# Where a projection's bias is added: a product with one row of ones, or an addition on VectorE while PSUM is emptied

## The chip, the cores and the metric

The kernel runs on one core of a Trainium2 chip. It uses TensorE (PE, with its weight loads shown as PEld), VectorE (DVE), ScalarE (ACT), GpSimd (POOL) and the DMA engines, whose transfers are started by SyncE (SP) and GpSimd. The metric is the device time of one execution in microseconds (us), lower is better.

## The reference, cut to what matters

The program is eight blocks, each added to the node features `x` (3125 nodes, 256 features, float32), over a graph of 53125 edges. Five times in it a matrix of node features is multiplied by a weight matrix and the result stays in node order. Three of the five have a bias, and two of those a rectifier:

```python
h = jnp.einsum('ni,hio->hno', x, W)          # block 0: 256 columns + 8 folded ones, no bias
logits = tokens @ router_w.T                 # block 1: 8 columns, no bias
logits = xt @ Wr + br                        # block 5: 8 columns, bias
h = jax.nn.relu(x @ w1 + b1)                 # block 6, twice: 256 columns, bias, rectifier
msg = ew[:, None] * h[src]                   #   then gathered by edge and summed by node
```

## The kernel before

Nodes lie in 25 tiles of 125 (`T` = 25, `P` = 125), worked through in five groups (`NG`) of five (`GT`). The transposed features `XT` (or `F`) have features on partitions, in `KH` = 2 halves of 128, and nodes along the free dimension.

The program is a sequence of phases (`Phase`), and each ends with a barrier of all engines (L79 to L81), so nothing of one phase overlaps the next. `project` is one such phase. It is called five times: at about 64 us (block 0), 1552 us (block 1), 4691 us (block 5), 5388 us and 6203 us (block 6, first and second convolution). In each call:

- SyncE loads the weights (L514), the bias as one row of one partition (`b_row`, L516), and in block 0 two vectors that are broadcast to 128 partitions (L518).
- VectorE waits for all loads and then copies each node tile of `XT` into one of five slots (L541), since TensorE takes its stationary operand from there. Before it refills a slot it waits until the product that used it is done (`multiplied`).
- TensorE waits for the slot (`slot_ready`) and for its PSUM bank to be free (`kept`), multiplies the two halves (L559), and where there is a bias adds a third product, of a row of ones with the bias row (L562). Each float32 product is two passes, so a tile is four weight loads with four matmul records, and two more of each with a bias. Only then it signals `multiplied`.
- ScalarE waits for `multiplied`, reads the PSUM bank, applies the rectifier or a copy, and writes the tile into `H` or `logits` (L571), and signals `kept`.
- In blocks 0 and 6 SyncE waits for each group of five tiles and stores it to a table in DRAM (L523), 625 KB at a time, and at the end waits until all five stores have landed.

There are five slots and five PSUM banks (`acc`), one for each tile of a group, so up to five tiles may be under way. After the projections of block 6 comes `aggregate`, whose first instruction on VectorE is the clearing of `AT` (L612). After that of blocks 1 and 5 comes the routing of tokens, whose first instruction is an iota on GpSimd (L1131).

`normalize` (L379) makes `XT` and is used below for comparison: in block 2 it stores the same table of 625 KB groups (L411).

Of the kernel before, what the change touches and what calls it, by code (L numbers as in the profile page):

```python
# [23 lines left out]
ALU = mybir.AluOpType  # L24
ACT = mybir.ActivationFunctionType
# [5 lines left out]
P = 125  # L31
T = N // P
CH = E // P
KH = C // 128
GT = 5
NG = T // GT
# [73 lines left out]
def tile(t):  # L110
    return bass.ds(t, 1)


def nodes(t, n=1):
    return bass.ds(t * P, n * P)
# [372 lines left out]
def project(nc, g, XT, weight, out, bias=None, relu=False, table=None, fold=(), att=None):  # L488

    width = weight.shape[-1]
    extra = sum(heads for heads, _ in fold)
    full = width + extra
    with Phase(nc) as ph:
        w = ph.sb("w", [128, KH, full])
        vec = ph.sb("vec", [128, max(len(fold), 1), width])
        prod = ph.sb("prod", [128, width])
        b_row = ph.sb("b_row", [1, width])
        slot = ph.sb("slot", [128, GT, KH, P])  # L500
        acc = ph.psum("acc", [P, GT, 512])
        loaded = ph.sem("loaded")
        folded = ph.sem("folded")
        slot_ready = ph.sem("slot_ready")
        multiplied = ph.sem("multiplied")
        kept = ph.sem("kept")
        stored = ph.sem("stored")
        n_loads = 1 + (bias is not None) + len(fold)
        n_folds = sum(2 * KH for _ in fold)
        block = ph.block()  # L510

        @block.sync
        def _(sp):
            sp.dma_start(w[:, :, 0:width], weight.rearrange("(h p) n -> p h n", p=128)).then_inc(loaded, 16)  # L514
            if bias is not None:
                sp.dma_start(b_row[:], bias).then_inc(loaded, 16)  # L516
            for n, (_, v) in enumerate(fold):
                sp.dma_start(vec[:, n], v.partition_broadcast(128)).then_inc(loaded, 16)  # L518
            if table:
                with sp.Fori(0, NG) as i:  # L520
                    sp.wait_ge(kept, (i + 2) * GT)
                    for dram, lo, n in table:
                        sp.dma_start(dram[bass.ds(i * GN, GN), :].rearrange("(t p) c -> p t c", p=P),  # L523
                                     out[:, bass.ds(i * GT, GT), lo:lo + n]).then_inc(stored, 16)
                sp.wait_ge(stored, 16 * NG * len(table))

        @block.vector
        def _(dve):
            dve.wait_ge(loaded, 16 * n_loads)
            then = Steps(dve, folded)  # L530
            at = width
            for n, (heads, _) in enumerate(fold):
                for h in range(KH):
                    then(dve.tensor_tensor(prod[:], w[:, h, 0:width], vec[:, n], ALU.mult))
                    then(dve.tensor_reduce(w[:, h, at:at + heads], prod[:].rearrange("p (a c) -> p a c", a=heads), AX_X, ALU.add))
                at += heads
            with dve.Fori(0, NG) as i:
                for k in range(GT):

                    dve.wait_ge(multiplied, i * GT + k + 1)  # L540
                    dve.tensor_copy(slot[:, k], XT[:, :, nodes(i * GT + k)]).then_inc(slot_ready, 1)  # L541
            if att is not None:
                dve.wait_ge(kept, GT + T)
                then(dve.tensor_copy(att[:], out[:, :, full - HEADS:full]))

        @block.tensor
        def _(pe):

            pe.sem_inc(multiplied, GT)
            pe.wait_ge(loaded, 16 * n_loads)  # L550
            if n_folds:
                pe.wait_ge(folded, n_folds)
            with pe.Fori(0, NG) as i:
                for k in range(GT):
                    pe.wait_ge(slot_ready, i * GT + k + 1)

                    pe.wait_ge(kept, i * GT + k + 1)
                    for h in range(KH):
                        last = pe.matmul(acc[:, k, 0:full], slot[:, k, h], w[:, h], start=(h == 0),  # L559
                                         stop=(h == KH - 1 and bias is None))  # L560
                    if bias is not None:
                        last = pe.matmul(acc[:, k, 0:width], g.ones[0:1, :], b_row[:], start=False, stop=True)  # L562
                    last.then_inc(multiplied, 1)

        @block.scalar
        def _(act):
            act.sem_inc(kept, GT)
            with act.Fori(0, NG) as i:
                for k in range(GT):
                    act.wait_ge(multiplied, (i + 1) * GT + k + 1)  # L570
                    act.activation(out[:, tile(i * GT + k), :].rearrange("p a c -> p (a c)"), acc[:, k, 0:full],  # L571
                                   ACT.Relu if relu else ACT.Copy).then_inc(kept, 1)


def aggregate(nc, g, table, AT):
# [1885 lines left out]
def build(nc, arrays, begin=0, end=8):  # L2461
# [9 lines left out]
    with ExitStack() as top:  # L2471
# [4 lines left out]
        if begin <= 0 < end:  # L2476
            normalize(nc, g, X, XT)
            with ExitStack() as st:
                a_dst = st.enter_context(nc.sbuf_tensor("a_dst", [P, T, HEADS], F32))
                with ExitStack() as s2:  # L2480
                    H = s2.enter_context(nc.sbuf_tensor("H", [P, T, C + 2 * HEADS], F32))
                    project(nc, g, XT, d["L0_gnn_W"], H, fold=((HEADS, d["L0_gnn_a_src"]), (HEADS, d["L0_gnn_a_dst"])),
                            table=((edge_table, 0, C + HEADS),), att=a_dst)
                attend_edges(nc, g, edge_table, a_dst, d["dst_flat"], dst_row, X)
            count_edges(nc, g, counts, scratch)
        if begin <= 1 < end:
            with ExitStack() as st:
                XN = st.enter_context(nc.sbuf_tensor("XN0", [P, T, C], F32))
                logits = st.enter_context(nc.sbuf_tensor("logits0", [P, T, NX], F32))
                normalize(nc, g, X, XT, XN)  # L2490
                project(nc, g, XT, d["L0_ffn_router"], logits)
                sparse_experts(nc, g, logits, XN, X, scratch, K=2, guard=1e-12, keep=True, hidden=C,
                               **{name: d["L0_ffn_" + name] for name in ("w1", "b1", "w2", "b2")})
# [28 lines left out]
        if begin <= 5 < end:  # L2522
            with ExitStack() as st:
                XN = st.enter_context(nc.sbuf_tensor("XN2", [P, T, C], F32))
                logits = st.enter_context(nc.sbuf_tensor("logits2", [P, T, NX], F32))
                normalize(nc, g, X, XT, XN, twice=True)
                project(nc, g, XT, d["L2_ffn_Wr"], logits, bias=d["L2_ffn_br"])
                sparse_experts(nc, g, logits, XN, X, scratch, K=2, hidden=4 * C, w1=d["L2_ffn_W1"], b1=d["L2_ffn_b1"],
                               w2=d["L2_ffn_W2"], b2=d["L2_ffn_b2"], gain=d["L2_ffn_ln_g"], offset=d["L2_ffn_ln_b"])
# [38 lines left out]
```

## Time and profile before

| | us |
|---|---|
| median of 3 runs | 7331.43 |
| lowest, highest | 7329.41, 7336.07 |
| the profiled execution's own time | 7337.61 |
| its span, first to last instruction | 7336.1 |
| mean granted TensorE clock | 0.768 of 2.4 GHz |

The profile is of one execution. Its busy shares are means over stages that are limited by different engines: TensorE 67%, its weight loads 56%, VectorE 37%, ScalarE 32%, GpSimd 34%. A change in one stage has to be read from that stage. The granted clock is 1.00 at 2.4 GHz and 0.50 at 1.2 GHz.

### The profile page before, as it was taken

How to read it: one execution, taken by the hardware profiler on the slowest of the kernel's cores; microseconds unless marked ns; L12 is line 12 of the kernel's file. 1: busy time of each engine (PE TensorE's matmuls, PEld its weight loads, DVE VectorE, ACT ScalarE, POOL GpSimd, SP SyncE). 2: the span in 40 equal slices, each digit the busy share in tenths (PEclk: the TensorE clock that was granted, in tenths of full speed). 3: DMA queues.
4: the chain of work that ended last, by engine and by line, in shares of the span. 5: the costliest groups of instructions: out<-in, count | busy, mean ns of one | idle time of the engine just before them, and what ended most of it. 6: DMA issues, size and time to landing. Idle time of an engine off the chain costs nothing. (4 is left out here: it accounts for less than half of the span.)

```text
span 7336.1 us, 100226 instructions
## 1 busy us (share of the span) xinstructions
PE 4950.6 (67%) x23535; PEld 4095.8 (56%) x23536; DVE 2728.1 (37%) x5564; ACT 2374.0 (32%) x4829; POOL 2524.9 (34%) x2090
## 2 busy tenths in 40 slices
PE   3878635535357677584989989559757766766746
PEld 2766535523245554483878868558635554555535
DVE  4444535530222212105968879400022222222143
ACT  2333124424211113343656656335311112111132
POOL 3778300022357760201000000030127773577600
PEclk7887769968766668797999989679856666576668
DMA  3333220012223320221111111022113331233300
GB/s 88 95 98 99 73 76 34 34 36 84 69 77 85 85 72 6 76 79 47 57 41 52 43 50 57 10 85 81 53 45 85 85 85 44 68 85 85 76 13 19
DMA packets 360158, 464.62 MB, mean 63 GB/s; under 512 B 191387, under 2 KB 275146, under 8 KB 360074
## 3 DMA queue, kind: packets, MB, share of 16 engines
q0 software_dynamic: 262016, 293.64, 15.8%
q1 hardware_dynamic: 79988, 152.25, 6.0%
q10 hardware_dynamic: 18070, 17.79, 0.9%
q8 instruction: 31, 0.51, 0.0%
q14 instruction: 53, 0.43, 0.0%
HBM read 377.19 MB, written 84.20 MB: 63 GB/s over the span
## 5 line engine op out<-in xcount | busy, mean ns | idle before, releaser
L607 POOL DMA_INDIRECT p_message<-node_table,p_index x1275 | 1554.5, 1219 | 737.0 <-ACT p_index L599 461.4
L641 PE MATMUL p_acc<-p_spread,p_message 125*128 125x160 f32 x5100 | 1357.8, 425 | 644.1 <-DVE p_spread L621 300.0
L641 PEld LDWEIGHTS p_acc<-p_spread,p_message 125*128 125x128 f32 x5100 | 1101.4, 276 | 901.1 <-issue 827.3
L2158 PE MATMUL p_acc<-p_H,p_eT 125*125 125x256 f32 x3750 | 823.5, 378 | 0.0
L1131 POOL IOTA p_order_i<- 125x200 int32 x3 | 1.1, 374 | 2359.0 <-SPq L79 2359.0
L599 ACT COPY p_index<-src_col 125x1 int32 x1275 | 240.5, 191 | 1682.4 <-PE p_acc L641 1508.4
L2158 PEld LDWEIGHTS p_acc<-p_H,p_eT 125*125 125x125 f32 x3750 | 695.0, 187 | 106.0
L886 POOL DMA_INDIRECT p_message<-edge_table,p_index x425 | 562.5, 1324 | 144.9 <-issue 128.0
L627 DVE TENSOR_TENSOR AT<-AT,p_acc 128x320 f32 x75 | 36.6, 488 | 1314.1 <-PE p_acc L641 920.1
L621 DVE TENSOR_SCALAR p_spread<-node_number,dst_value,edge_weight_col 125x160 f32 x1275 | 397.0, 385 | 198.7 <-issue 198.7
L1439 PE MATMUL p_up<-p_xT,p_w1s 128*128 128x125 f32 x3056 | 393.6, 287 | 101.9 <-ACT p_xT L1474 73.3
L1439 PEld LDWEIGHTS p_up<-p_xT,p_w1s 128*128 128x128 f32 x3056 | 379.7, 201 | 133.6 <-ACT p_xT L1474 67.9
L1079 PE MATMUL p_acc<-p_message,p_spread 125*125 125x260 f32 x1666 | 424.4, 421 | 6.7 <-DVE p_message L1013 3.6
L729 PE MATMUL p_acc<-p_cell,p_low 125*125 125x325 bf16 x1250 | 231.6, 337 | 257.0 <-DVE p_cell L707 182.5
L1494 DVE TENSOR_TENSOR p_rows_out<-p_down,p_b2s 125x256 f32<-125x256 f32 x136 | 57.7, 425 | 921.6 <-PE p_down L1448 840.7
L1079 PEld LDWEIGHTS p_acc<-p_message,p_spread 125*125 125x125 f32 x1666 | 347.2, 210 | 79.7 <-issue 12.6
L1448 PE MATMUL p_down<-p_w2s,p_hid 128*125 128x256 f32 x1528 | 364.9, 388 | 3.0 <-ACT p_hid L1479 2.3
L483 PE MATMUL p_turned<-identity,p_slot 125*128 125x125 f32 x400 | 88.9, 374 | 411.0 <-DVE p_slot L451 407.2
L1479 ACT ACTIVATE p_hid<-p_up,p_b1s 128x125 f32<-128x125 f32 x764 | 272.6, 365 | 243.2 <-PE p_up L1439 200.0
L729 PEld LDWEIGHTS p_acc<-p_cell,p_low 125*125 125x125 bf16 x1250 | 176.1, 152 | 284.6 <-issue 230.7
L2081 ACT ACTIVATE p_eT<-p_turned 125x500 f32<-125x500 f32 (+1 forms) x525 | 251.1, 540 | 203.6 <-PE p_turned L2151 187.2
L1448 PEld LDWEIGHTS p_down<-p_w2s,p_hid 128*125 128x125 f32 x1528 | 283.2, 193 | 45.5 <-ACT p_hid L1479 7.5
(400 smaller groups left out, 6913.7 us busy)
## 6 DMA issues: line engine op xcount, KB each, us to landing
p_count<-edge_counts SPq DMA_DIRECT2D x75, 762.9 KB
p_message<-node_table,p_index POOLq DMA_INDIRECT x1275
edge_counts<-p_total SPq DMA_DIRECT2D x25, 762.9 KB
p_rows_in<-dealt ACTq DMA_DIRECT2D x139, 125.0 KB
made<-p_rows_out SPq DMA_DIRECT2D x136, 125.0 KB
p_w1s<-in_L_ffn_W POOLq DMA_DIRECT2D x16, 1024.0 KB
p_dst_all<-dst_row SPq DMA_DIRECT2D x25, 531.2 KB
p_w2s<-in_L_ffn_Wd POOLq DMA_DIRECT2D x8, 1024.0 KB
```

What stands on the lines that cost most here:

```text
L599: act.copy(index[:, k:k + 1], g.src[:, bass.ds(r * R_CH + k, 1)]).then_inc(index_ready, 1)
L607: pool.indirect_dma_start(message[:, k, :], None, table, bass.IndirectOffsetOnAxis(ap=index[:, k:k + 1], axis=0)).then_inc(message_ready[k ...
L621: dve.tensor_scalar(spread[:, k], g.iota[:, window], g.dstf[:, bass.ds(r * R_CH + k, 1)], g.weight[:, bass.ds(r * R_CH + k, 1)], ALU.is_eq ...
L641: last = pe.matmul(acc[:, h, 0:WIN], message[:, k, h * 128:(h + 1) * 128], spread[:, k], start=(k == 0), stop=(k == R_CH - 1))
L729: last = pe.matmul(at[:, h, 0:n * T], low[:, k], cell[:, k, d:d + n].rearrange("p d h -> p (d h)"), start=start, stop=False)
L886: pool.indirect_dma_start(message[:, m, k, :], None, table, bass.IndirectOffsetOnAxis(ap=index[:, m, k:k + 1], axis=0)).then_inc(landed[m] ...
L1079: last = pe.matmul(at, spread[:, k], message[:, m, k], start=(k == 0), stop=(k == R_CH - 1))
L1439: last = pe.matmul(up[:, c % 4, 0:UN], w1s[:, s, h, c * 128:(c + 1) * 128], xT[:, h], start=(h == 0), stop=(h == KH - 1))
L1448: last = pe.matmul(down[:, a, 0:C], hid[:, c, a * P:(a + 1) * P], w2s[:, s, c], start=(c == 0), stop=(c == HC - 1))
L1479: act.activation(hid[:, c], up[:, c % 4, 0:UN], ACT.Gelu, bias=b1s[:, s, c:c + 1]).then_inc(hid_ready, 1)
L2081: act.activation(eT[:, r % 4, 0:n], turned[:, r % 4, 0:n * P].rearrange("p (a n) -> p a n", a=n), ACT.Copy).then_inc(run_kept, 1)
L2158: last = pe.matmul(acc[:, s, 0:C], eT[:, r % 4, a % 4], H[:, a, 0:C], start=(a == 0), stop=(a == T - 1))
```

## The change

In the three projections with a bias the third product is gone. The bias is loaded to all 125 partitions (`b_all`). VectorE reads the PSUM bank, adds `b_all` and writes the tile into the output; this signals `added`, for which TensorE waits before it uses the bank again. Where there is a rectifier, ScalarE applies it in place, in a loop of one tile per turn, and signals `kept`, for which the store waits. Where there is none, `added` is `kept`, and ScalarE has nothing to do. VectorE's program becomes: fill the five slots, then for each later tile add for the tile five before it and refill that tile's slot, and at the end five additions. The two projections without a bias keep their code.

```diff
-        b_row = ph.sb("b_row", [1, width])
+        b_all = ph.sb("b_all", [P, width])
...
+        added = ph.sem("added") if bias is not None and relu else kept
...
-                sp.dma_start(b_row[:], bias).then_inc(loaded, 16)
+                sp.dma_start(b_all[:], bias.rearrange("a c -> (a c)").partition_broadcast(P)).then_inc(loaded, 16)
...
-            with dve.Fori(0, NG) as i:
+
+            def feed(i, k):
+                dve.tensor_copy(slot[:, k], XT[:, :, nodes(i * GT + k)]).then_inc(slot_ready, 1)
+
+            def add(i, k):
+                dve.wait_ge(multiplied, (i + 1) * GT + k + 1)
+                dve.tensor_tensor(out[:, tile(i * GT + k), :].rearrange("p a c -> p (a c)"), acc[:, k, 0:width], b_all[:], ALU.add).then_inc(added, 1)
+
+            if bias is None:
+                with dve.Fori(0, NG) as i:
+                    for k in range(GT):
+                        dve.wait_ge(multiplied, i * GT + k + 1)
+                        feed(i, k)
+            else:
+                dve.wait_ge(multiplied, GT)
                 for k in range(GT):
-
-                    dve.wait_ge(multiplied, i * GT + k + 1)
-                    dve.tensor_copy(slot[:, k], XT[:, :, nodes(i * GT + k)]).then_inc(slot_ready, 1)
+                    feed(0, k)
+                with dve.Fori(1, NG) as i:
+                    for k in range(GT):
+                        add(i - 1, k)
+                        feed(i, k)
+                for k in range(GT):
+                    add(NG - 1, k)
...
-                    pe.wait_ge(kept, i * GT + k + 1)
+                    pe.wait_ge(added, i * GT + k + 1)
                     for h in range(KH):
-                        last = pe.matmul(acc[:, k, 0:full], slot[:, k, h], w[:, h], start=(h == 0),
-                                         stop=(h == KH - 1 and bias is None))
-                    if bias is not None:
-                        last = pe.matmul(acc[:, k, 0:width], g.ones[0:1, :], b_row[:], start=False, stop=True)
+                        last = pe.matmul(acc[:, k, 0:full], slot[:, k, h], w[:, h], start=(h == 0), stop=(h == KH - 1))
                     last.then_inc(multiplied, 1)
...
+            if bias is None:
+                with act.Fori(0, NG) as i:
+                    for k in range(GT):
+                        act.wait_ge(multiplied, (i + 1) * GT + k + 1)
+                        act.activation(out[:, tile(i * GT + k), :].rearrange("p a c -> p (a c)"), acc[:, k, 0:full],
+                                       ACT.Relu if relu else ACT.Copy).then_inc(kept, 1)
+            elif relu:
+                act.sem_inc(added, GT)
+                with act.Fori(0, T) as t:
+                    act.wait_ge(added, t + GT + 1)
+                    o = out[:, tile(t), :].rearrange("p a c -> p (a c)")
+                    act.activation(o, o, ACT.Relu).then_inc(kept, 1)
```

## Rows read from the trace of the kernel before

**Rows 1.** The page: busy time by engine, and the costliest group.

```profile
PE 4950.6 (67%) x23535; PEld 4095.8 (56%) x23536; DVE 2728.1 (37%) x5564; ACT 2374.0 (32%) x4829; POOL 2524.9 (34%) x2090
...
L607 POOL DMA_INDIRECT p_message<-node_table,p_index x1275 | 1554.5, 1219 | 737.0 <-ACT p_index L599 461.4
```

**Rows 2.** Line L562: its matmuls (ns min/median/max), and who waited for them.

```profile
L562 PE MATMUL p_acc<-p_b_row,ones x150: 352/626/786, 4694.1 to 6284.1; 1*125 1x256 f32 x100, 1*125 1x8 f32 x50
...
  ACT H L571: 147.8, 50
```

**Rows 3.** Timeline, block 6's first projection, its start (start us, duration us).

```profile
5388.76 0.31 SPq L516 DMA_DIRECT2D p_b_row<-in_L_gnn_c_b  x1
5391.48 1.15 DVE L541 COPY p_slot<-XT 128x250 f32 x5 [4.91 <-DMA p_b_row<-in_L_gnn_c_b]
...
5391.83 2.07 PE L559 MATMUL p_acc<-p_w,p_slot 128*125 128x256 f32 x4 [4.76 <-DVE p_slot L541]
...
5393.83 1.21 PE L562 MATMUL p_acc<-p_b_row,ones 1*125 1x256 f32 x2
...
5394.97 2.07 PE L559 MATMUL p_acc<-p_w,p_slot 128*125 128x256 f32 x4
```

**Rows 4.** Timeline, the same projection: its stores, and the next phase's first VectorE instruction.

```profile
5408.41 63.05 SPq L523 DMA_DIRECT2D node_table<-H  x5
...
5480.48 5.53 DVE L612 MEMSET AT<- 128x6570 f32 x1 [25.34 <-issue]
```

**Rows 5.** Waits of SyncE in that projection (us in total, times, longest).

```profile
SPq L79 <- DMA node_table<-H: 6.4, 1, 6.4
```

**Rows 6.** Timeline, block 5's projection (8 columns, bias): first products, next phase.

```profile
4693.18 1.00 PE L559 MATMUL p_acc<-p_w,p_slot 128*125 128x8 f32 x4 [5.37 <-DVE p_slot L541]
...
4730.61 0.37 POOL L1131 IOTA p_order_i<- 125x200 int32 x1 [1382.01 <-SPq L79]
```

**Rows 7.** Timeline, block 1's projection (8 columns, no bias): products, next phase.

```profile
1554.19 21.17 PE L559 MATMUL p_acc<-p_w,p_slot 128*125 128x8 f32 x100 [5.23 <-DVE p_slot L541]
...
1576.38 0.39 POOL L1131 IOTA p_order_i<- 125x200 int32 x1 [709.78 <-SPq L79]
```

**Rows 8.** Timeline, block 0's projection (264 columns, no bias, two broadcast loads).

```profile
64.46 0.42 SPq L518 DMA_DIRECT2D p_vec<-in_L_gnn_a_dst  x1
67.84 0.42 DVE L534 TENSOR_TENSOR p_prod<-p_w,p_vec 128x256 f32<-128x256 f32 x1 [6.08 <-DMA p_vec<-in_L_gnn_a_dst]
...
72.13 25.38 PE L559 MATMUL p_acc<-p_w,p_slot 128*125 128x264 f32 x100 [9.88 <-DVE p_slot L541]
...
80.54 20.66 SPq L523 DMA_DIRECT2D edge_table<-H  x5
```

**Rows 9.** Windows: busy us (count) of each engine, granted clock, DMA share, GB/s.

```profile
76.20:78.00 1.80, 1.80 (x6) 1.35 (x5) 0.33 (x2) 0.43 (x2) 0.00 (x0) 0.51 0.00 0
78.00:80.00 2.00, 2.00 (x11) 1.69 (x10) 0.65 (x3) 0.85 (x3) 0.00 (x0) 1.00 0.00 0
...
5391.40:5470.00 78.60, 78.17 (x150) 41.10 (x150) 6.98 (x25) 9.19 (x24) 0.00 (x0) 0.50 0.09 33
```

**Rows 10.** Timeline, block 2's normalize: its five stores, and the next phase.

```profile
2034.87 18.37 SPq L411 DMA_DIRECT2D node_table<-XN  x5
...
2065.59 5.53 DVE L612 MEMSET AT<- 128x6570 f32 x1 [21.73 <-issue]
```

**Rows 11.** Waits of SyncE in that normalize.

```profile
SPq L79 <- DMA node_table<-XN: 9.9, 1, 9.9
```

**Rows 12.** Single lines: an addition out of PSUM, ScalarE from SBUF to SBUF, its table loads.

```profile
L1494 DVE TENSOR_TENSOR p_rows_out<-p_down,p_b2s x136: 423/425/426, 1695.6 to 5275.1; 125x256 f32<-125x256 f32 x136
...
L2180 ACT ACTIVATE p_slot<-R x75: 398/400/417, 3789.7 to 4656.2; 125x256 f32 x75
L2180 ACT ACT_TABLE_LOAD  x15: 1283/1283/1283, 3788.4 to 4653.6; - x15
```

**Rows 13.** Timeline, block 4: five additions on VectorE in a row.

```profile
4643.68 1.77 DVE L2213 TENSOR_TENSOR X<-X,p_slot 125x256 f32 x5 [2.93 <-ACT p_slot L2180]
```

More of the change, by code:

```diff
@@ L567, in _ @@
             act.sem_inc(kept, GT)
[L568 to L572, printed above, removed]
+            if bias is None:
[10 more added lines that the diff above has]
+                    act.activation(o, o, ACT.Relu).then_inc(kept, 1)
 def aggregate(nc, g, table, AT):
```

## The prediction

> **What bounds the kernel now.** I read the page first. No engine bounds the whole: TensorE is busy 67% of the span, and the costliest group is GpSimd's gather of messages, 1554.5 us of 7336.1 [rows 1]. The phases are cut off from each other by barriers, so the question is how much shorter the three changed phases get, and whether anything outside them moves.
>
> Then line L562, the product with one row. There are 150 matmul records of it, two for each of 75 tiles, and ScalarE waited 147.8 us for them in the two projections of block 6 [rows 2]. The timeline shows the order: in those projections a tile's main product starts at 5391.83, its bias product at 5393.83 and the next tile at 5394.97, so a tile takes 3.14 us, 2.00 for the main product and 1.14 for the bias [rows 3]. That pattern repeats for 25 tiles and in the second convolution. TensorE is busy 78.17 of 78.60 us, VectorE 6.98 and ScalarE 9.19, all at a granted clock of 0.50 [rows 9]. TensorE bounds these phases; after its last tile come the last store and the barrier. From the first product to the next phase's first VectorE instruction are 5480.48 - 5391.83 = 88.65 us [rows 3, 4]. In block 5 the same stretch takes 4730.61 - 4693.18 = 37.43 us [rows 6].
>
> The two projections without a bias run the program that TensorE will run after the change, and I take its pace from them.
>
> **Block 5 (8 columns).** The projection without a bias takes 1576.38 - 1554.19 = 22.19 us from its first product to the next phase's first GpSimd instruction [rows 7]. The difference is 15.2 us. VectorE's addition replaces ScalarE's copy behind the last product; on 8 columns neither can be a large cost, and the 256-column addition, 0.425 us [rows 12], is an upper bound.
>
> **Block 6, TensorE.** In block 0 the 25 tiles of 264 columns take 25.38 us [rows 8]. The granted clock was 0.51 in the window up to 78.00 us and 1.00 in the next, that is, it rose from 1.2 to 2.4 GHz some 5.9 us after the first product [rows 8, 9]. If slow work is half as fast, those 5.9 us count as 2.9 us of fast work, so the 25 tiles are 25.4 - 5.9 + 2.9 = 22.4 us of fast work: 0.90 us a tile, 0.87 for 256 columns (by 256/264). At 1.2 GHz a tile is then twice that, 1.75 us; the 2.00 us of now [rows 3] include the change-over from the bias product, and bound it from above.
>
> Does the clock rise here? Now it does not: it is 0.50 over 78.60 us of a TensorE that is 99% busy [rows 9]. What differs from block 0 is the product with one row in every tile, 1.14 of 3.14 us [rows 3]. After the change the instructions are those of block 0 but for 8 columns, so I take its rise. The Trainium skill (TensorE: Matmul & The Clock Gate, Part 1: The HAM clock gate) says that the gate goes by how busy the array has recently been, and that activity releases it. By that rule the clock rises after the change, as I forecast; but by the same rule it should be high now as well, and there this case's trace disagrees, with 0.50 at 99% busy. If what holds it down now stays after the change, the time is that of the first rival below.
>
> **Block 6, the stores.** With the clock up, a group of five tiles is done in 4.4 us, and the stores no longer keep pace. Now the last store is issued at 5408.41 + 63.05 = 5471.46 at the latest, waits 6.4 us to land [rows 4, 5] and the next phase starts 2.6 us after that (5480.48 - 5477.86). The same stores issued faster than they land are seen in block 2: first issue 2034.87, last issue done at 2053.24, landed 9.9 us later at 2063.14, next phase at 2065.59 [rows 10, 11]. So five stores that queue behind each other take 28.3 us from the first issue and 2.5 us more to the next phase. That is the new bound. The first issue comes when the first group is through: 80.54 - 72.13 = 8.4 us after the first product in block 0 [rows 8], plus the addition's place in the chain (0.425 us [rows 12]), less the narrower tile (0.2): 8.7 us. Sum: 8.7 + 28.3 + 2.5 = 39.5 us in place of 88.65, 49.1 us less, twice: 98.2 us. The computing itself ends near 25.38 x 256/264 + 0.5 (handing over) + 0.425 + 0.400 = 25.9 us, and the fifth store's turn comes only at about 8.7 + 4 x 5.3 = 29.9 us (26.5 us for five, from 28.3 less some 1.8 of latency). So there are 4 us to spare on the computing side.
>
> **VectorE and ScalarE.** Per tile VectorE has an addition and a copy. Five additions of SBUF operands in a row took 1.77 us, so 0.34 from start to start [rows 13]; five copies 1.15 us, so 0.22 [rows 3]. Together 0.56 us; with no overlap at all 0.425 + 0.29 = 0.72 us. Both are under 0.87, so TensorE hides them. Wherever VectorE would need over (29.9 - 7) / 20, about 1.1 us a tile, it would show. The copy queued behind each addition waits for the product of the same slot, as it does now, so no new wait arises; TensorE has four more tiles ready. ScalarE's pass in place goes SBUF to SBUF, 0.400 us for this shape [rows 12], inside 0.87, and its loop turn per tile has the other 0.47 us. TensorE waits for the addition only.
>
> **The bias load.** In place of one row 125 rows are loaded. Now the first copy comes 5391.48 - 5389.07 = 2.4 us after the issue's end; in block 0, behind two such broadcasts, 67.84 - 64.88 = 3.0 us, and the issue takes 0.42 in place of 0.31 [rows 3, 8]. Between 0 and 0.7 us, all of it on the path, as nothing of the phase starts before. I take 0.7 in block 6 (same shape) and 0.3 in block 5 (8 columns): 1.7 us.
>
> **The sum.** 15.2 + 98.2 - 1.7 = 111.7 us. The profiled span of 7336.1 would become 7224.4. The profiled execution's own time, 7337.61, is 6.2 us over the median shown, 7331.43; both lose the same, so the median becomes 7219.7, some 7220.
>
> Nothing outside the three phases changes its code. `aggregate` starts after the barrier in either case, on gathers paced by GpSimd [rows 1], and I cost it at nothing. If its gathers lost or won 0.2%, that would be 3 us, and I let the range hold it. VectorE's program grows by some ten instructions per call. No row prices the loading of instructions; I take zero, since the 2.5 us from a barrier to the next work [rows 10, 11] come with long programs too, and those 2.5 us once more per call would be the upper end.
>
> **Rivals.**
> *The clock stays at 1.2 GHz in block 6.* For it: it did for 78.60 us [rows 9], and in block 1 TensorE's 100 passes of 8 columns give no sign of a rise, 0.84 us a tile as the 21.17 us show [rows 7]. Against it: block 0, the same work, rose within 5.9 us. Then TensorE bounds: 25 x 1.75 = 43.8, + 0.5 + 0.425 + 0.400 + 0.3 to the issue of the last store = 45.4, + 0.3 + 6.4 + 2.6 = 54.7 us, so 34.0 us less in place of 49.1. Median 7220 + 30 = 7250.
>
> *ScalarE reloads its table in each turn of its new loop.* The loop of L2180 did so, once per turn, 15 loads of 1.283 us for three calls of five turns [rows 12]. With 25 turns ScalarE needs 1.283 + 0.400 + some 0.1 = 1.8 us a tile, 45 us for all, from 2.5 us on; then 0.3 + 0.3 + 6.4 + 2.6: 57 us, 32 us less per phase. Median 7220 + 34 = 7254. Against it: that loop holds a Gelu, and the rectifier of now is in a loop too, and ScalarE's 24 instructions in its window are 9.19 us busy, 0.383 each, with no room for a load of 1.283 [rows 9].
>
> *One tile in flight: slower.* If each product waited until the tile before had been added, rectified and its slot refilled, a tile would be 2.07 (record) + 0.2 + 0.425 + 0.400 + 0.29 + handing over (3 x 0.06) = 3.57 us, over the 3.14 of now by 0.43, 10.7 us per phase of block 6; in block 5 1.00 + 0.2 + 0.2 + 0.29 + 0.1 = 1.8 against 1.45, 8 us. Median 7331 + 21 + 8 + 2 = 7362. It decides only when the round of one tile, divided by the tiles in flight, exceeds 3.14 us; with two in flight it is 1.8 already. Five slots and five banks speak against it.
>
> **How the numbers follow.** The forecast as worked out has 0.82, the low clock 0.10, the table load 0.02, one tile in flight 0.01; 0.05 is left for something unseen in the later phases, of either sign, mostly still faster. A difference of 0.2% (14.7 us) is about what can be told from none. So faster 0.97, same 0.01, slower 0.02. The range: the sum may be too small by 1.7 (a free load) and 4 us (runs differ by 7 us among themselves, and the first store may come earlier), 7212 with rounding; above, it takes in the low clock, 7250. The forecast's own range is 7212 to 7228.
>
> **What would show it.** In the changed profile: no L562 row; in block 5 about 22.5 us from first product to the next phase; in block 6 a clock that is 0.50 for the first 4 to 8 us and 1.00 after, about 39 to 40 us to the clearing of `AT`, SyncE's last wait near 10 us in place of 6.4, tiles 0.87 us apart; no table load in ScalarE's loop; VectorE's addition at 0.42 to 0.43 us; the bias load landing 2.4 to 3.0 us after its issue. Wrong would make it: a clock that stays low (first of all), a store queue that drains slower than block 2's, or a shift in `aggregate`.

## The result, and the profile after

The changed kernel takes 7225.99 us (median of 4 runs, 7222.10 to 7229.17), against 7332.12 for the kernel before (4 runs, 7329.41 to 7336.07): a ratio of 0.9855, 95% interval 0.9841 to 0.9869, 106 us less. The forecast was 7220 with a range of 7212 to 7250. The profiled execution after took 7222.10 us with a span of 7220.5.

The page after, first its busy times and then the gathers of `aggregate`. No busy share has moved by more than one percent of the span, since the shares are means over the whole program:

```profile
PE 4826.3 (67%) x23385; PEld 4039.1 (56%) x23386; DVE 2752.3 (38%) x5639; ACT 2373.2 (33%) x4804; POOL 2529.2 (35%) x2090
...
L630 POOL DMA_INDIRECT p_message<-node_table,p_index x1275 | 1558.8, 1223 | 639.1 <-ACT p_index L622 357.2
```

TensorE has 150 matmuls less (23535 to 23385) and 124.3 us less busy time [rows 1]. The timeline of the first projection of block 6 after the change, from its loads to the next phase (start us, duration us, engine, line), to be held against [rows 3, 4]:

```profile
5368.43 0.42 SPq L515 DMA_DIRECT2D p_w<-in_L_gnn_c_w  x1
5368.90 0.35 SPq L517 DMA_DIRECT2D p_b_all<-in_L_gnn_c_b  x1
5372.18 1.09 DVE L540 COPY p_slot<-XT 128x250 f32<-128x250 f32 x5 [5.46 <-DMA p_b_all<-in_L_gnn_c_b]
5372.52 23.35 PEld L578 LDWEIGHTS p_acc<-p_w,p_slot 128*125 128x125 f32 x100 [5.55 <-DVE p_slot L540]
5372.52 23.75 PE L578 MATMUL p_acc<-p_w,p_slot 128*125 128x256 f32 x100 [5.32 <-DVE p_slot L540]
5374.77 0.42 DVE L544 TENSOR_TENSOR H<-p_acc,p_b_all 125x256 f32 x1 [1.51 <-PE p_acc L578]
5375.11 0.28 DVE L540 COPY p_slot<-XT 128x250 f32 x1
5375.33 0.42 ACT L595 ACTIVATE H<-H  x1 [7.60 <-DVE H L544]
...
5380.43 17.66 SPq L524 DMA_DIRECT2D node_table<-H  x5
...
5396.32 0.42 DVE L544 TENSOR_TENSOR H<-p_acc,p_b_all 125x256 f32<-125x256 f32 x1 [0.44 <-PE p_acc L578]
5396.87 0.42 ACT L595 ACTIVATE H<-H  x1 [0.45 <-DVE H L544]
5410.75 5.53 DVE L635 MEMSET AT<- 128x6570 f32 x1 [14.01 <-issue]
```

All 100 matmuls are one row of 23.75 us: TensorE has no gap any more. Its work ends at 5396.3, ScalarE's at 5397.3, and then nothing computes for 13.5 us until `AT` is cleared. What SyncE waited for in that gap is in its waits (us in total, times, longest):

```profile
SPq L79 <- DMA node_table<-H: 10.2, 1, 10.2
```

The windows of the same stretch (busy us and count of PE, PEld, DVE, ACT and POOL, then granted clock, DMA share and GB/s), to be held against the window of 78.60 us at 0.50 in [rows 9]:

```profile
5375.00:5376.00 1.00, 1.00 (x4) 0.81 (x3) 0.40 (x2) 0.42 (x1) 0.00 (x0) 0.50 0.00 0
5376.00:5377.00 1.00, 1.00 (x5) 0.80 (x5) 0.53 (x2) 0.00 (x0) 0.00 (x0) 0.79 0.00 0
5377.00:5378.00 1.00, 1.00 (x7) 0.86 (x6) 0.64 (x3) 0.42 (x1) 0.00 (x0) 1.00 0.00 0
5378.00:5396.00 18.00, 18.00 (x85) 15.59 (x83) 12.36 (x39) 8.75 (x21) 0.00 (x0) 1.00 0.28 97
```

The clock rose about 4 us after the first product and stayed at 2.4 GHz. Before the change it did not rise in this phase.

To compare kernels I use the length of a phase, from the issue of its weight load to the next phase's first instruction, because the whole program also moves for other reasons. For the first convolution that is 5480.48 - 5388.30 = 92.18 us before and 5410.75 - 5368.43 = 42.32 us after. The last column is the sum of everything outside the three phases.

| | block 5 | block 6, first | block 6, second | rest of the span |
|---|---|---|---|---|
| before | 39.91 | 92.18 | 91.88 | 7112.1 |
| after | 25.42 | 42.32 | 43.20 | 7109.6 |

The three phases lost 14.5 + 49.9 + 48.7 = 113.0 us, and the rest 2.6 us, together the 115.6 us between the two spans. The medians differ by 106: the profiled execution before, at 7337.61, was 5.5 us over the median of its kernel, and the one after 3.9 us under the median of its own.

### The profile page after: what moved, and what is told of

It reads as the page before. It is cut to its first block and busy times, and to the rows that moved or that the text cites. A ratio compares the mean times of both kernels' runs of the same rounds, so it can differ in the third digit from the quotient of the medians.

```text
span 7220.5 us, 100024 instructions
## 1 busy us (share of the span) xinstructions
PE 4826.3 (67%) x23385; PEld 4039.1 (56%) x23386; DVE 2752.3 (38%) x5639; ACT 2373.2 (33%) x4804; POOL 2529.2 (35%) x2090
## 5 line engine op out<-in xcount | busy, mean ns | idle before, releaser
L2181 PEld LDWEIGHTS p_acc<-p_H,p_eT 125*125 125x125 f32 x3750 | 695.4, 187 | 106.1
```

The lines of the kernel that those rows point to most:

```text
L2181: last = pe.matmul(acc[:, s, 0:C], eT[:, r % 4, a % 4], H[:, a, 0:C], start=(a == 0), stop=(a == T - 1))
```

## The experiments

The totals of the kernel before in the later series were 7329.6, 7331.4, 7330.1 and 7330.4 us; a ratio is always to the runs beside it. The phases of each row are from one profile (us):

| | total, us | ratio to before | block 5 | block 6, first | block 6, second |
|---|---|---|---|---|---|
| before, again | 7332.8 (one run) | | 39.60 | 92.09 | 91.86 |
| changed, again | 7218.8 | 0.9845 (0.9832 to 0.9859) | 25.38 | 42.15 | 43.29 |
| before, bias product over 128 rows | 7237.3 | 0.9874 (0.9859 to 0.9889) | 35.11 | 48.43 | 48.78 |
| changed, bias product kept | 7335.5 | 1.0006 (0.9997 to 1.0015) | 40.46 | 93.08 | 93.71 |
| changed, no bias at all | 7206.7 | 0.9833 (0.9819 to 0.9846) | 24.67 | 41.46 | 41.80 |
| changed, one store of five | 7194.9 | 0.9811 (0.9796 to 0.9826) | 25.39 | 30.75 | 31.51 |
| changed, three additions | 7223.4 | 0.9848 (0.9833 to 0.9863) | 25.74 | 45.44 | 45.42 |
| changed, one tile in flight | 7335.2 | 1.0006 (0.9996 to 1.0015) | 38.18 | 94.15 | 94.28 |
| changed, stores 1 and 3 from ScalarE | 7217.9 | 0.9847 (0.9833 to 0.9860) | 25.39 | 42.69 | 43.43 |
| changed, stores 1 and 3 from GpSimd | 7194.3 | 0.9811 (0.9798 to 0.9824) | 25.38 | 39.95 | 44.01 |
| the same in block 0 alone | 7200.4 | 0.9825 (0.9812 to 0.9838) | 25.39 | 42.28 | 42.78 |

### Is it the single row that holds the clock down?

```diff
 # on the kernel before
-        b_row = ph.sb("b_row", [1, width])
+        b_row = ph.sb("b_row", [128, width])      # cleared by GpSimd, then row 0 loaded
...
-                        last = pe.matmul(acc[:, k, 0:width], g.ones[0:1, :], b_row[:], start=False, stop=True)
+                        last = pe.matmul(acc[:, k, 0:width], g.ones[:, :], b_row[:], start=False, stop=True)
```

> The kernel before, but the third product runs over all 128 rows: 128 rows of ones with a matrix whose first row is the bias and whose other rows are zero. Same number of products and columns. Theory: it is the product with a single row that keeps TensorE at 1.2 GHz in block 6. Then the granted clock rises to 1.00 some 5 us after the first product, a tile takes 6 passes of 0.215 = 1.29 us, the store queue is no longer than its pace (6.5 us a group), and from first product to the clearing of AT it is about 36 + 0.3 + 6.4 + 2.6 = 45 us in place of 88.65: total some 86 us under before, near 7246. Rival, the change between the two kinds of product (another stationary operand, another tile) keeps the clock down: still 0.50 and 3.14 us a tile, total 7332. In block 5 (8 columns) both expect 0.50.

Measured: 7237.3 us, and phases of 48.4 and 48.8 us. The same six passes per tile, with 128 rows in the last two, and the clock rises. Two windows of this kernel, and a tile of it once the clock is up:

```profile
5380.00:5382.00 2.00, 2.00 (x8) 1.64 (x7) 0.17 (x1) 0.18 (x1) 0.00 (x0) 0.66 0.00 0
...
5384.00:5411.00 27.00, 27.00 (x127) 23.52 (x126) 4.95 (x17) 8.04 (x21) 0.00 (x0) 1.00 0.26 89
```

```profile
5383.90 0.83 PEld L566 LDWEIGHTS p_acc<-p_w,p_slot 128*125 128x125 f32 x4
...
5384.76 0.40 PEld L569 LDWEIGHTS p_acc<-p_b_row,ones 128*125 128x125 f32 x2
...
5385.19 0.83 PEld L566 LDWEIGHTS p_acc<-p_w,p_slot 128*125 128x125 f32 x4
```

A tile takes 5385.19 - 5383.90 = 1.29 us, as expected, against 3.14 before [rows 3]. So the product's own passes are the small part of its cost: padding it with 127 rows of zeros, without taking any work away, gives 92 us (7329.6 to 7237.3) of the 106 to 113. Block 5 also shortened, from 39.6 to 35.1 us, at a clock of 0.50 in both, with the same 150 matmuls of 8 columns. Its 25 tiles thus lose some 0.18 us each with a single-row product that a full-row one doesn't.

The rival is refuted in part only. Another stationary operand every few passes doesn't hold the clock down, since this kernel still has it. But padding took away a second thing beside the single row. First the weight loads before the change, where TensorE goes over to the other kind of product, and then the bias products of two tiles of the padded kernel while its clock was still 0.50:

```profile
5393.83 0.49 PEld L562 LDWEIGHTS p_acc<-p_b_row,ones 1*125 1x125 f32 x2 [0.65 <-issue]
5394.97 1.34 PEld L559 LDWEIGHTS p_acc<-p_w,p_slot 128*125 128x125 f32 x4 [0.65 <-issue]
```

```profile
5378.24 1.06 PE L569 MATMUL p_acc<-p_b_row,ones 128*125 128x256 f32 x2
...
5380.80 0.88 PE L569 MATMUL p_acc<-p_b_row,ones 128*125 128x256 f32 x2
```

Before the change the weight loads stood idle for 0.65 us at each of the two changes in a tile; in the padded kernel these stops are gone, and at the same low clock a tile takes 5380.80 - 5378.24 = 2.56 us in place of 3.14. So the 99% that the profile calls busy hide 0.58 us a tile. Whether the clock was held down by passes over a single row or by these stops is not shown: no run of a projection of 256 columns has the one without the other.

### Is anything gained by VectorE and ScalarE?

```diff
 # on the changed kernel
+                    if bias is not None:
+                        last = pe.matmul(acc[:, k, 256:256 + width], g.ones[0:1, :], b_all[0:1, :], start=True, stop=True)
                     last.then_inc(multiplied, 1)
```

> The changed kernel, and TensorE still runs the product of a row of ones with one row of the bias, into columns of the bank that nobody reads. So everything moved to VectorE and ScalarE is there, and only the removal of the product is undone. Theory: all the gain is TensorE's, the additions and the pass in place are hidden. Then 3.14 us a tile at clock 0.50, 88.65 + 0.5 for the addition's place in the last tile, + 0.5 to 0.7 for each bias load: total 7332 + 3 = 7335, not told from before. Rival, part of the gain comes from emptying PSUM sooner (VectorE): total under 7320.

Measured: 7335.5 us, no difference from before, and phases of 93.1 and 93.7 us, 1 to 2 us over those of before. The window shows the old state, with TensorE busy 78.57 of 79.00 us at 0.50:

```profile
5389.00:5468.00 79.00, 78.57 (x150) 41.10 (x150) 15.25 (x49) 9.99 (x24) 0.00 (x0) 0.50 0.09 33
```

The whole gain is the product's removal. What the other engines were given, with the wider load of the bias, costs 0.9 to 1.8 us per phase of block 6.

> The changed kernel with no bias at all in the three projections: no load of it, no addition; ScalarE applies the rectifier while it reads PSUM. It leaves out the bias of the three projections. It prices what is left of the bias in the changed kernel. Theory: one addition's place in the first group (0.4 to 0.5 us) and 0.5 us or more of the load, per phase: block 6 phases 1 to 1.5 us shorter each, block 5 about 1; total 3 to 4 us under the changed kernel, 7222. Rival, VectorE's additions slow TensorE or the stores: each block 6 phase is 3 us shorter or more.

The edit is `bias = None` at the head of `project`. The phases are 0.7, 0.9 and 1.4 us shorter than in the changed kernel: that is all that is left of the bias, about as expected. The total, 7206.7, is not: 7218 to 7219 was expected, and it is 12 us under what the phases alone give against 7222. A part of it may be data: the stage from block 5's routing to block 6 takes 651.7 us in place of 658.2, and without the bias the router has other logits. That is not shown; the rest lies in stretches that the edit doesn't touch, and stays open.

### What bounds the phases now?

```diff
 # on the changed kernel
-                with sp.Fori(0, NG) as i:
+                with sp.Fori(0, 1 if relu else NG) as i:
...
-                sp.wait_ge(stored, 16 * NG * len(table))
+                sp.wait_ge(stored, 16 * (1 if relu else NG) * len(table))
```

> The changed kernel with only the first of the five table stores made in each projection of block 6; the other four groups' rows of the table are left out, so the gathers read what block 2 left there. Theory: after the change the stores bound these phases. Without them a phase ends with ScalarE's last pass, 28.9 us after the weight load's issue, + 2.6: 31.5 us in place of 42.3 and 43.2; total some 22 us less, 7204. Rival, TensorE or the chain through ScalarE is still the bound: under 3 us less in each.

Measured: 30.75 and 31.51 us, within 1 us of the 31.5 expected. The last pass of ScalarE and the clearing of `AT`:

```profile
5398.58 0.42 ACT L595 ACTIVATE H<-H  x1 [0.45 <-DVE H L544]
5401.13 5.53 DVE L635 MEMSET AT<- 128x6570 f32 x1 [2.67 <-issue]
```

The idle time behind the last pass is 2.1 us where it was 13.5. So four of the five stores cost 11.6 and 11.7 us in the changed kernel; before the change they ran beside a slower TensorE. The total is 27 us under the changed kernel's 7222 (median of its nine runs), 23.3 of it from these phases.

> The changed kernel with two further additions of the same shape on VectorE behind each real one, into spare tiles. It tests the point from which VectorE would show, put at some 1.1 us a tile. VectorE then needs 3 x 0.34 + 0.22 = 1.24 us a tile at the least, 1.5 us if the starts overlap less. Theory: 25 tiles take 31 to 38 us, the fifth store is 3 to 8 us later than its turn, and each phase of block 6 is 3 to 9 us longer (45 to 52 us); block 5 (8 columns, additions of 0.17 us, TensorE 0.84 a tile) longer by under 5. Total 7232 to 7248. Rival, VectorE has more to spare than thought: no change, 7226.

```diff
 # in add(), behind the real addition
+                for d in range(2):
+                    dve.wait_ge(idle[d], i * GT + k + 1)
+                    dve.tensor_tensor(spare[:, d], b_all[:], b_all[:], ALU.add).then_inc(idle[d], 1)
```

Measured: the real additions come 1.20 us apart (5388.77, 5389.97, 5391.18), and now TensorE waits for its slots:

```profile
5388.77 0.43 DVE L546 TENSOR_TENSOR H<-p_acc,p_b_all 125x256 f32 x1
5388.92 0.72 PEld L585 LDWEIGHTS p_acc<-p_w,p_slot 128*125 128x125 f32 x4 [0.48 <-DVE p_slot L542]
...
5389.97 0.42 DVE L546 TENSOR_TENSOR H<-p_acc,p_b_all 125x256 f32 x1
```

The phases are 3.1 and 2.2 us longer than in the changed kernel, at and below the lower end of what was expected, and the total, 7223.4, is under the 7232 to 7248 expected and can't be told from the changed kernel's. SyncE's last wait shows where the bound lies:

```profile
SPq L79 <- DMA node_table<-H: 6.5, 1, 6.5
```

It was 10.2 us in the changed kernel and 6.4 before the change [rows 5]. So at 1.20 us a tile, where it was 0.87, the last store no longer queues: most of the 8 us that 25 tiles lose were hidden by the stores, and 2 to 3 us show. The threshold of 1.1 us was about right.

> The changed kernel, and TensorE in the three projections also waits, before each tile, until the tile before is kept (added and rectified). It is the slower rival of the prediction made on purpose. From the changed profile a round is 2.25 us (first product to addition, at 1.2 GHz) + 0.56 (addition to the pass in place) + 0.42 + 0.1 = 3.3 us, against 3.14 before; in block 5 1.3 to 1.5 against 1.45. Theory: slower than the changed kernel by 50 us or more in each phase of block 6 if the clock stays at 0.50, phases of 93 to 97 us and a total of 7335 to 7350; if the clock rises even so, a round is 2.3 us, phases of 68 to 72 us and a total near 7295.

```diff
                     pe.wait_ge(added, i * GT + k + 1)
+                    if bias is not None:
+                        pe.wait_ge(kept, (i + 1) * GT + k)
```

Measured: 7335.2 us, phases of 94.2 and 94.3 us. The chain of a tile, and the window over 79 us of it:

```profile
5400.97 2.07 PE L580 MATMUL p_acc<-p_w,p_slot 128*125 128x256 f32 x4 [1.20 <-ACT H L597]
5403.19 0.42 DVE L544 TENSOR_TENSOR H<-p_acc,p_b_all 125x256 f32 x1 [2.62 <-PE p_acc L580]
5403.53 0.28 DVE L540 COPY p_slot<-XT 128x250 f32 x1
5403.74 0.42 ACT L597 ACTIVATE H<-H  x1 [2.83 <-DVE H L544]
5404.21 1.34 PEld L580 LDWEIGHTS p_acc<-p_w,p_slot 128*125 128x125 f32 x4 [1.90 <-ACT H L597]
```

```profile
5381.00:5460.00 79.00, 50.74 (x99) 28.71 (x100) 15.23 (x49) 9.98 (x24) 0.00 (x0) 0.50 0.09 33
```

A round is 5404.21 - 5400.97 = 3.24 us. No single-row product is left, and the clock stays at 0.50 all the same, with TensorE busy 50.74 of 79.00 us. The total is no different from before: with one tile in flight the removal of the product is worth nothing. The five slots and banks let the tiles overlap.

### Can the stores be sped up?

```diff
 # on the changed kernel: SyncE stores groups 0, 2, 4, another engine 1 and 3
-                with sp.Fori(0, NG) as i:
+                for i in range(0, NG, 2):
...
+            @block.gpsimd
+            def _(pool):
+                for i in range(1, NG, 2):
+                    pool.wait_ge(kept, (i + 2) * GT)
+                    for dram, lo, n in table:
+                        pool.dma_start(dram[bass.ds(i * GN, GN), :].rearrange("(t p) c -> p t c", p=P),
+                                       out[:, bass.ds(i * GT, GT), lo:lo + n]).then_inc(stored2, 16)
+                pool.wait_ge(stored2, 16 * (NG // 2) * len(table))
```

> The changed kernel with the table stores of the projections dealt in turn to SyncE's queue (groups 0, 2, 4) and GpSimd's (1, 3). Theory: in block 6 the stores of one queue are the bound at 1.2 to 2.4 GHz of TensorE (28 us for five, of which the computing needs 25); with two queues the last store starts when the last group is ready, 25 us after the first product, and the next phase at 25 + 0.3 + 6.4 + 2.6 = 34 us in place of 38 to 39; block 0 from 42 to about 36. Together some 13 us less, 7213. Rival, 121 GB/s is what the engines or DRAM give to rows of 1 KB whatever the number of queues: no change, 7226. Second rival, GpSimd's queue is slower in the making of its descriptors (its direct loads elsewhere are large): 0 to 10 us more.

> The changed kernel with stores 1 and 3 of each projection issued by ScalarE's queue in place of SyncE's, its loops unrolled for it. Two queues gave 7194 with GpSimd's queue, 32 us under the changed kernel, of which the profile shows only some 6 us in the projections; the rest was in gathers that took 1202 ns in place of 1214. Theory: the two parts are separate. With ScalarE's queue the projections of block 6 take 34 to 39 us (load to next phase) in place of 42 to 43 and block 0's less by some 5; the gathers, whose program is GpSimd's alone, are at 1211 to 1214, and the total is 7226 - 10 to 20 = 7206 to 7216. Rival, the gathers follow the queues: 1202 ns and a total near 7194 again.

Measured: with GpSimd 7194.3 us, the fastest kernel here and one that leaves nothing out, 28 us under the changed kernel, where 13 were expected; with ScalarE 7217.9, no better than the changed kernel's 7215 to 7229, and above the 7206 to 7216 expected. The DMA rates over the first projection of block 6, a stretch of 36 us in 40 equal slices, first with ScalarE's queue and then with GpSimd's, show why:

```profile
GB/s 0 0 0 9 0 40 96 119 119 122 118 121 121 119 122 122 121 119 121 122 122 119 121 121 119 122 119 121 116 94 112 119 122 121 122 76 9 0 0 0
```

```profile
GB/s 0 0 0 9 0 0 69 105 121 121 121 122 53 85 85 99 160 190 225 216 129 119 131 84 75 139 187 203 213 193 126 116 76 6 0 0 0 18 0 0
```

SyncE's and ScalarE's queues together give the same 121 GB/s as SyncE's alone. Beside GpSimd's queue the rate reaches 225. Even so the three projections with a table are only 6.4 us shorter together with GpSimd's stores (block 0 from 51.12 to 46.30 us, then 42.32 to 39.95, and 43.20 to 44.01), and only 4.6 us against the changed kernel's second profile, whose block 0 took 49.40. My 34 us for a phase was wrong, with either queue, and what the two queues gain in rate reaches the end of the phase only in part. Most of the rest is in the gathers, which the edit doesn't touch: GpSimd spent 1556.3 us on the 1275 gathers of `aggregate` in the changed kernel's second profile and 1537.9 here, and 563.6 and 556.4 on the 425 of block 0, 25.6 us less. How much of that is on the path was not measured. The gather's row, its ns as min/median/max, here and in the changed kernel's second profile:

```profile
L641 POOL DMA_INDIRECT p_message<-node_table,p_index x1275: 1180/1202/5029, 2059.1 to 6801.2; - x183
```

```profile
L630 POOL DMA_INDIRECT p_message<-node_table,p_index x1275: 1207/1212/5000, 2062.5 to 6823.0; - x183
```

> The changed kernel with the stores dealt between SyncE's and GpSimd's queue in block 0 alone; both projections of block 6 store as in the changed kernel. With all three dealt the total was 7194, 28 us under 7222, but the three projections were only some 6 us shorter together and the rest lay in gathers of 1202 ns (1211 to 1214 in the other profiles). Theory: the gathers' time follows GpSimd's program or its queue as a whole, so two stores in block 0 are enough: gathers near 1202 ns, total 7222 - 5 - 15 to 20 = 7197 to 7202. Rival, each stretch follows the stores just before it: gathers of block 6 at 1211 to 1214 and a total of 7222 - 5 = 7217.

Measured: 7200.4 us, a median gather of 1205 ns, and phases of block 6 like the changed kernel's. So with two stores by GpSimd in block 0 the gathers of phases thousands of us later are shorter. It goes with GpSimd's program or its queue as a whole, not with the stores just before. The medians by phase show that it isn't one shift of all gathers: in the changed kernel they are 1212 or 1214 ns in every phase, here 1191 in block 0, 1209 in block 2 and 1200 in both convolutions of block 6, and with stores by GpSimd in all three projections 1191, 1209, 1196 and 1196. Another instruction in GpSimd's program is not enough: the padded kernel, where GpSimd clears the bias's rows, has 1211 ns. By what means they shorten is open; whether it is how the program lies, and not the stores, no run tries.

### How much of a difference is the execution?

> The changed kernel once more, unchanged. It asks whether the stretches outside the three phases belong to the program or to the execution. In the profiles so far they differ by up to 29 us between programs (7112 us before, 7110 changed, 7088 without a bias), and the gather of messages on GpSimd has a median of 1211 ns before, 1214 changed, 1202 with two queues. Theory: the gather's time belongs to the program, so it is 1214 again, and the phases are 25.4, 42.3 and 43.2 us (load to next phase) again; total 7222 to 7229. Rival, it belongs to the execution: a median of 1211 or 1202 and a total 5 us or more away from 7226.

> The kernel before once more, with a profile of its own. Theory: the gather's median is 1211 ns again and the phases are 39.9, 92.2 and 91.9 us; the stretches outside them differ from the first profile's by no more than the runs differ, 5 us. Rival: they differ by more, so that one profile of each kernel can't tell a shift outside the phases.

The first is the changed kernel, the second the kernel before. Measured: the three phases repeat within 0.3 us. Block 0's projection doesn't: 51.12 and 49.40 us in the changed kernel, 50.97 and 49.88 in the one before, and it goes with when the clock rose there (by windows of 1 us, 6.1 and 2.9 us after the first product, and 5.8 and 4.0). The rest of the span was 7103.4 us in the changed kernel's second profile where it was 7109.6 in the first, and 7107.7 before where it was 7112.1. The changed kernel's gather median was 1212 ns, after 1214: the 1214 was the execution's, and I had taken it for the program's. The second series of the changed kernel has a median of 7218.8 us, 112.6 under the 7331.4 beside it, the first had 106.1. All nine runs of it have a median of 7222.1.

## Why the prediction was right, point by point

**TensorE bounds the phases.** Right for the kernel before, and shown by the kept product: with everything else changed, the time is that of before.

**Block 5.** 14.9 us were forecast (15.2 less 0.3), 14.5 measured. The difference is the bias load: the first copy came 4687.78 - 4685.62 = 2.2 us after the issue's end, 0.8 later than before, not 0.3.

**The clock rises.** Right, 3.9 and 4.9 us after the first product in the two phases. The 5.9 us of [rows 9] were one execution's: in its second profile the kernel before took 4.0 us in the same place, so this moment moves by some 2 us by itself. That the product with one row held the clock down is shown by its removal and by its padding; whether the single row did it, or the stops of 0.65 us beside it, is not. The Trainium skill (TensorE: Matmul & The Clock Gate, Part 1: The HAM clock gate) has the gate go by how busy the array is. The run with one tile in flight agrees (0.50 at 64% busy, full rows); the kernel before and the one with the product kept disagree, if busy is what the profile calls busy (0.50 at 99%, single rows), and so does block 5 of the changed kernel (0.50 over 20.80 us of matmuls of 8 columns over full rows, busy all the time). The forecast took the profile's share for the rule's, and the 2.56 us of a padded tile show that the share hides 0.58 of 3.14 us. So the busy time of the profile alone doesn't tell the clock here; what else counts, no run shows.

**The stores become the bound.** Right. From the first product to the clearing of `AT` 39.5 us were forecast and 5410.75 - 5372.52 = 38.2 measured, and 38.7 in the second convolution. The first store was issued at 7.9 and 8.4 us, not 8.7: the clock rose earlier than in [rows 9]. That is the execution's luck, and in the changed kernel's second profile it was 7.7 and 8.6. In the first convolution, from there to the last landing, it took 17.66 + 10.2 = 27.9 us, not 28.3. To take the queue's drain from block 2, where the same bytes are stored, is what made this term good.

**VectorE and ScalarE are hidden.** Right. The addition took 0.425 us as in [rows 12], the pass in place 0.417 where 0.400 was taken; three additions cost 3.1 and 2.2 us a phase.

**The bias load.** 0.7 us was taken for block 6; it was 0.5 in the first projection (2.9 in place of 2.4 us from the issue's end) and 1.0 in the second. All three together are 2.4 us against the 1.7 forecast.

**The sum.** 111.7 us forecast, 113.0 in the phases, 106.1 and 112.6 in the medians of two series. The assumption that the rest adds nothing holds within what one kernel does by itself: the rest moves by 4 to 6 us from one execution to the next, so the 6 us between 7220 and 7226 have no cause in the change that I can show. That the phases came out within 1.3 us of the forecast is in part luck, since the first store alone moves by 0.9 us between the four phases with the moment of the clock's rise.

**The rivals.** None came. The table load isn't there: ScalarE's passes are 0.87 us apart. One tile in flight was priced at 7362 and measured at 7335: I had put the slot's refill in the round, which runs beside the pass in place, and had one handing-over too many (3.57 us for 3.24). In block 5 it was to cost 8 us and the phase was 1.7 us shorter than before. Even with one tile in flight the kernel would not have been slower. The cost of the low clock as a rival, 54.7 us per phase, was not tried by itself.

## What to carry to other kernels

A product with one row is not a free way to add a bias on TensorE: look at the granted clock of the stretch, not at the product's own time. Here a TensorE that the profile calls 99% busy ran at half its clock beside it, and most of the gain could be had by giving it full rows. When the bound of a phase goes, ask which queue runs beside it: the stores that were hidden took back some 11.6 us of each phase, and could be priced beforehand from a phase that stores the same bytes faster. And judge a change of 1% by the lengths of the phases that it touches, since the others wander by several us.

## What the runs showed of the hardware that was not expected

- The clock stayed at 1.2 GHz in two different ways: 99% busy with one third of the matmuls on a single row, and 64% busy with full rows. It also stayed there over 20.80 us of matmuls of 8 columns over full rows without a gap (block 5 after the change). With full rows of 256 or 264 columns and no gaps it rose 2.9 to 6.1 us after the first product, by amounts that differed between executions of one kernel.
- A single-row product costs more than one over 128 rows of the same columns, at the same clock: block 5 took 39.6 us with the one and 35.1 with the other. In block 6, at 0.50, a tile of six passes took 3.14 us with the one and 2.56 with the other, and each change between the two kinds left the weight loads idle for 0.65 us ("issue"), which the busy share of TensorE doesn't show.
- SyncE's and ScalarE's queues gave 121 GB/s together, as SyncE's does alone; with GpSimd's beside it the rate reached 225 GB/s.
- The gathers' own time on GpSimd fell from 1212 to 1202 or 1205 ns (median of 1275) in the two programs in which GpSimd also issued plain stores of the tables, and the totals fell by 22 to 28 us, of which the three projections with a table are 4.6 to 6.5. Why is open.
